# Values of the first attention issued for three key tiles at a time, with six tiles of probabilities held

## The chip, the cores and the metric

One Trainium2 chip, one of its cores. The metric is the device time of one execution in microseconds (us). It is told as the median of several runs, and one execution of its own is profiled.

## The reference

Four sequences x of 256 rows by 512 columns (float32), each with a context of 1601 rows by 512 columns, go through four residual steps:

```
x = x + latent_attention(layernorm(x), ctx)       # 16 heads of 32, low-rank: Wq_d, W_qk, Wkv_d, Wv_u
x = x + layernorm(x) @ dequantised_int4(W0).T + bias
x = x + grouped_attention(layernorm(x), ctx)      # 16 query heads of 96, 4 key/value heads
x = x + mixture(layernorm(x))                     # dense product plus a rank-32 path with expert weights
```

The change concerns the first step. There, for every head, scores = (C_q @ W_qk) @ C_kv^T / sqrt(32) over the 1601 context rows, attn = softmax(scores), and the result is attn @ C_kv @ Wv_u, with C_kv = ctx @ Wkv_d of 32 columns.

## The kernel before, in words

The program runs four blocks one after the other: products of the context, the latent attention with the quantised layer, the grouped attention, and the mixture. Only `latent_attention_and_ffn` (L663 to L1179) is touched.

It works in 16 stages, S = 4 sequences by 4 groups of 4 heads. A stage has 13 key tiles of 128 keys (the last has 65), and 1024 queries (4 heads by 256 rows) in two halves of 512 columns.

- TensorE, `scores(s, kt)` (L900): two matmuls with operands in fp32r (L909), one for each half, into one of three PSUM banks taken in turn (SB = 3). From the fourth half on it waits until the exponential of three halves earlier has read its bank (L908).
- ScalarE, `probs(s, kt)` (L1025): two exponentials (L1031), each from a bank into half of a tile of probabilities `pr`. There are NPR = 4 such tiles, and before tile n it waits for the values of tile n - NPR (L1028).
- TensorE, `values(s, kt)` (L914): two products with operands in float32 (L922), with 64 columns of `cv` as weights, one to partitions 0 to 63 and one to 64 to 127 of the same bank, summed over the stage. The trace shows each as two MATMUL records, so four for a tile.
- The rest of TensorE's work goes through a ring of four PSUM banks (`ring_item`, L956), whose banks are read by VectorE or ScalarE in the same order: 32 maxima of the next stages' scores a stage (L970 on TensorE in fp32r, L1132 on VectorE), the row of shifts (`row`, L974 and L93), and in some stages `raise` (L979), transposes (`xt`, `xat`, L952), `cq` (L989), `a` (L994), `ffn` (L1004), all these in float32, and `q` (L931, products in fp32r). An item is issued once the item four places earlier has been read.
- The order of all this on TensorE is written out by `course(s)` (L772): the scores of the first two units of key tiles, then by turns the values of a unit and the scores of the unit after the next. `some(share)` lays ring items in between, 2 shares after each tile's scores and 3 after a unit's values. `total` is the number of shares of a stage, so the items are spread evenly whatever the units are. ScalarE follows the same order (L1069), VectorE follows the ring items alone.

So TensorE runs a stage as: scores 0 to 3, values 0 and 1, scores 4 and 5, values 2 and 3, and so on, to scores 12, values 10 and 11, the row, values 12.

Of the kernel before, what the change touches and what calls it, by code (L numbers as in the profile page):

```python
# [97 lines left out]
def build(nc, A, out):  # L98
# [10 lines left out]
    with ExitStack() as ctx:  # L109
        def sb(name, shape, dt=F32):  # L110
            return ctx.enter_context(nc.sbuf_tensor(name, shape, dt))

        ident = sb("ident", [P, P])
        negid = sb("negid", [QT, QT])
        ps = ctx.enter_context(nc.psum_tensor("ps", [P, 8 * BANK], F32))
        ln = {n: sb(f"ln_{n}", s) for n, s in
              (("st", [P, TT, 6]), ("mv", [P, TT, 2]), ("v", [P, TT]), ("t", [P, TT]), ("u", [P, TT]), ("y", [P, TT]))}
        h8all = sb("h8all", [P, B, NE])
        dlall = sb("dlall", [P, B, NE])
        w1T = sb("w1T", [P, DC, D])  # L120
        with ExitStack() as early:
            def weight(name, cols, dt=F32R):
                return early.enter_context(nc.sbuf_tensor(name, [P, DC, cols], dt))

            wkvh, wkvl = weight("wkvh", WV + WK), weight("wkvl", WV + WK)
            wqh, wql = weight("wqh", H1 * HD1), weight("wql", H1 * HD1)
            w0T = weight("w0T", D, F32)
            small = {n: early.enter_context(nc.sbuf_tensor(n, shape, F32)) for n, shape in
                     (("bias0", [P, D]), ("wqd", [P, DC, LQ]), ("wqk", [LQ, H0, 3 * HD0]), ("wvu", [P, NG * 2, 2, HD0 + 1]),
                      ("xa", [P, TT, D]), ("cq", [LQ, T]))}  # L130
            context_products(nc, A, ident, negid, ps, ln, wkvh, wkvl, wqh, wql, w0T, w1T, *small.values(),
                             k_scr, v_scr, cst_scr, cv_scr, wo_scr)
            latent_attention_and_ffn(nc, A, ident, negid, ps, ln, wkvh, wkvl, wqh, wql, w0T, *small.values(),
                                     cst_scr, cv_scr, q_scr, k_scr, v_scr, x_scr)
        grouped_attention(nc, A, ident, negid, ps, ln, q_scr, k_scr, v_scr, x_scr, y_scr, z_scr, wo_scr, w1T,
                          h8all, dlall)
        mixture(nc, A, ident, ps, y_scr, z_scr, h8all, dlall, out)
# [525 lines left out]
def latent_attention_and_ffn(nc, A, ident, negid, ps, ln, wkvh, wkvl, wqh, wql, w0T, bias0, wqd, wqk, wvu, xa, cq,  # L663
# [10 lines left out]
    keys = [P] * (KT - 1) + [last_rows]  # L674
    cuts = widths(NC, 4)
    NI = QT * len(cuts)
    UNITS = [(0, 1), (2, 3), (4, 5), (6, 7), (8, 9), (10, 11), (12,)]
    NPR = 4
    LEAD = 6
    NQ, NKL = H1 * HD1 // T, -(-WK // T)  # L680
    NU = NQ + NKL + TT
# [3 lines left out]
    with ExitStack() as ctx:  # L685
        def sb(name, shape, dt=F32):
            return ctx.enter_context(nc.sbuf_tensor(name, shape, dt))
# [12 lines left out]
        ast = sb("ast", [HD1 + QT, H0 * T], F32R)  # L700
        pr = sb("pr", [P, NPR, GC])
        osb = sb("osb", [P, BANK])
# [20 lines left out]
        def bank(i, n=BANK):  # L723
            return ps[:, i * BANK:i * BANK + n]
# [47 lines left out]
        def course(s):  # L772
            main, row, tail = beside(s)
            taken, given = [0], []
            total = 2 * KT + 3 * (len(UNITS) - 2)

            def some(share):
                taken[0] += share
                out = main[len(given):len(main) * taken[0] // total]
                given.extend(out)  # L780
                return out

            for t in UNITS[0]:
                yield "scores", s, t
                yield from some(2)
            for j, unit in enumerate(UNITS):
                for t in UNITS[j + 1] if j + 1 < len(UNITS) else ():
                    yield "scores", s, t
                    yield from some(2)
                for t in unit:  # L790
                    yield "values", s, t
                if j < len(UNITS) - 2:
                    yield from some(3)
                if j == len(UNITS) - 2:
                    assert len(given) == len(main)
# [103 lines left out]
        def _(pe):  # L899
# [14 lines left out]
            def values(s, kt):  # L914
# [5 lines left out]
                for half in range(2):  # L920
                    pe.wait_ge(exp_done, 2 * n + half + 1)
                    mm = pe.matmul(bank(OB)[64 * half:64 * half + 64, :], cv[0:keys[kt], b % 2, kt, :],  # L922
                                   pr[0:keys[kt], n % NPR, half * BANK:(half + 1) * BANK],
                                   start=(kt == 0), stop=(kt == KT - 1))
# [99 lines left out]
        def _(act):  # L1024
            def probs(s, kt):  # L1025
                n = s * KT + kt
                if n >= NPR:
                    act.wait_ge(av_mm, n - NPR + 1)  # L1028
                for half in range(2):
                    act.wait_ge(s_mm, 2 * n + half + 1)  # L1030
                    act.activation(pr[0:keys[kt], n % NPR, half * BANK:(half + 1) * BANK],  # L1031
                                   bank((2 * n + half) % SB)[0:keys[kt], :], ACT.Exp, scale=S0).then_inc(exp_done, 1)
# [792 lines left out]
```

## Time and profile before

| what | us |
|---|---|
| median of 3 runs | 2090.02 (2086.51 to 2091.49) |
| the profiled execution's own time | 2088.55 |
| its span, first to last instruction | 2086.8 |
| latent attention, its 16 stages | about 346 to 952 of the span |
| TensorE busy, whole span | 1940.6 |
| ScalarE busy, whole span | 948.3 |
| VectorE busy, whole span | 1119.8 |

Busy times are of one engine each and overlap. Matmuls are pipelined, so their recorded lengths overlap too. In a timeline, therefore, the time that a group of matmuls takes is read from its start to the start of the next group.

### The profile page before, as it was taken

What the parts mean: (1) busy time and instruction counts of PE and PEld (TensorE: products, weight loads), DVE (VectorE), ACT (ScalarE), POOL (GpSimd) and SP (SyncE); (2) the same over time, 40 slices, a digit from 0 to 9 for tenths busy, and PEclk for the clock granted to TensorE, in tenths of its full rate; (3) what the DMA queues carried; (4) which work ended last, traced back from release to release, by engine and by line L of the source; (5) the groups of instructions that cost most, each with busy time, mean ns of one, the idle gap of its engine ahead of it and who ended that gap; (6) DMA issues with size and microseconds to landing.
All of it is one profiled execution on the core that took longest, in us unless ns stands there. A gap on an engine that the chain in (4) does not pass through costs nothing. (4 is left out here: it accounts for less than half of the span.)

```text
span 2086.8 us, 23683 instructions
## 1 busy us (share of the span) xinstructions
PE 1940.6 (93%) x8690; PEld 1363.5 (65%) x8690; DVE 1119.8 (54%) x2093; ACT 948.3 (45%) x1826; POOL 652.4 (31%) x504
## 2 busy tenths in 40 slices
PE   6999989999999999996799999999999999999986
PEld 5999975444655555554567777677776677766752
DVE  2443326767656656642374555666556466664423
ACT  2322312444443444341256666646666566655540
POOL 0000000000000000000156676656766567655650
PEclk9999986999999999998789999999999999999985
DMA  6556731000101100010721222213222332202112
GB/s 179 161 175 205 234 105 39 1 12 16 64 25 34 51 31 16 31 41 26 190 56 43 71 73 73 74 44 84 62 64 60 84 84 62 69 16 55 36 26 95
DMA packets 109697, 149.51 MB, mean 72 GB/s; under 512 B 28777, under 2 KB 87529, under 8 KB 106510
## 3 DMA queue, kind: packets, MB, share of 16 engines
q1 hardware_dynamic: 101630, 145.36, 24.3%
q10 hardware_dynamic: 7952, 2.64, 0.6%
q8 instruction: 69, 1.13, 0.2%
q14 instruction: 46, 0.38, 0.1%
HBM read 96.52 MB, written 51.39 MB: 71 GB/s over the span
## 5 line engine op out<-in xcount | busy, mean ns | idle before, releaser
L1365 POOL TENSOR_TENSOR pl<-pf,ph 128x512 fp32r<-128x512 f32 (+1 forms) x480 | 640.1, 1352 | 350.2 <-ACT pf L1532 348.5
L1528 ACT ACTIVATE ph<-ps 128x512 fp32r<-128x512 f32 (+1 forms) x480 | 287.3, 599 | 350.8 <-PE ps L1436 350.0
L1591 DVE TENSOR_REDUCE pm<-ps 128x1 f32<-128x464 f32 (+1 forms) x512 | 320.9, 637 | 157.0 <-PE ps L1382 148.6
L1132 DVE TENSOR_REDUCE pm<-ps 128x1 f32<-128x400 f32 (+1 forms) x512 | 264.3, 569 | 99.8 <-PE ps L970 96.9
L1031 ACT ACTIVATE pr<-ps 128x512 f32<-128x512 f32 (+1 forms) x416 | 219.4, 601 | 192.8 <-PE ps L909 191.6
L1532 ACT ACTIVATE pf<-ps 128x512 f32<-128x512 f32 (+1 forms) x480 | 287.2, 598 | 2.4 <-POOL pl L1365 2.2
L1382 PE MATMUL ps<-kh,qh 96*128 96x464 f32 (+1 forms) x512 | 203.5, 404 | 21.0 <-DMA ql<-q_scr 12.9
L1354 POOL MEMSET vf<- 128x96 f32 x1 | 0.2, 178 | 708.3 <-POOLq L685 708.3
L1454 PE MATMUL ps<-pl,vh 128*97 128x512 f32 (+1 forms) x480 | 194.7, 406 | 20.9 <-POOL pl L1365 19.7
L922 PE MATMUL ps<-pr,cv 128*64 128x512 f32 (+1 forms) x832 | 207.2, 614 | 0.0
L1451 PE MATMUL ps<-ph,vh 128*97 128x512 f32 (+1 forms) x480 | 195.7, 408 | 4.8 <-ACT ph L1528 4.8
L1434 PE MATMUL ps<-qh,kh 104*128 104x512 f32 (+1 forms) x480 | 193.8, 404 | 1.4 <-issue 1.4
L1435 PE MATMUL ps<-qh,kl 96*128 96x512 f32 (+1 forms) x480 | 191.5, 399 | 0.0
L970 PE MATMUL ps<-cst,ast 96*128 96x400 f32 (+1 forms) x512 | 175.8, 403 | 16.4 <-DVE pm L1132 12.2
L1436 PE MATMUL ps<-ql,kh 96*128 96x512 f32 (+1 forms) x480 | 190.3, 396 | 0.0
L1452 PE MATMUL ps<-ph,vl 128*97 128x512 f32 (+1 forms) x480 | 189.6, 395 | 0.0
L970 PEld LDWEIGHTS ps<-cst,ast 96*128 96x128 f32 x512 | 96.5, 201 | 109.5 <-DVE pm L1132 46.8
L909 PE MATMUL ps<-ast,cst 104*128 104x512 f32 (+1 forms) x416 | 153.1, 431 | 5.5 <-ACT pr L1031 2.0
L1382 PEld LDWEIGHTS ps<-kh,qh 96*128 96x128 f32 x512 | 100.3, 196 | 64.5 <-DVE pm L1591 25.9
L1596 DVE SCALAR_TENSOR_TENSOR x<-ps,rec,x 128x512 f32<-128x512 f32 x128 | 96.0, 750 | 80.6 <-PE ps L1395 80.4
L1454 PEld LDWEIGHTS ps<-pl,vh 128*97 128x97 f32 (+1 forms) x480 | 78.2, 163 | 76.8 <-POOL pl L1365 47.5
L922 PEld LDWEIGHTS ps<-pr,cv 128*64 128x64 f32 (+1 forms) x832 | 51.6, 138 | 85.5 <-issue 58.3
(222 smaller groups left out, 2655.4 us busy)
## 6 DMA issues: line engine op xcount, KB each, us to landing
woT<-wo_turned SPq DMA_DIRECT2D x16, 1536.0 KB, 8.8
cnat<-in_ctx_dram SPq DMA_DIRECT2D x16, 768.0 KB
q_scr<-qst SPq DMA_DIRECT2D x48, 256.0 KB, 2.5
kf<-k_scr SPq DMA_DIRECT2D x16, 696.4 KB, 4.8
vf<-v_scr SPq DMA_DIRECT2D x16, 672.0 KB
v_scr<-vst SPq DMA_DIRECT2D x64, 144.0 KB, 2.2
k_scr<-kst SPq DMA_DIRECT2D x36, 192.0 KB, 4.6
wo_turned<-wo_out SPq DMA_DIRECT2D x32, 192.0 KB, 2.8
```

The source lines that it names most:

```text
L922: mm = pe.matmul(bank(OB)[64 * half:64 * half + 64, :], cv[0:keys[kt], b % 2, kt, :], pr[0:keys[kt], n % NPR, half * BANK:(half + 1) * BAN ...
L970: mm = pe.matmul(out[:, 0:k], ast[0:HD1, grp * GC + j * P:grp * GC + (j + 1) * P], cst[0:HD1, b % 2, k0:k0 + k], start=True, stop=True)
L1031: act.activation(pr[0:keys[kt], n % NPR, half * BANK:(half + 1) * BANK], bank((2 * n + half) % SB)[0:keys[kt], :], ACT.Exp, scale=S0).then ...
L1132: dve.reduce_max(pm[:, j, ch:ch + 1], src[:, 0:cuts[ch][1]], AX).then_inc(done["dve"], 1)
L1365: pool.tensor_tensor(pl[0:m, n % 2, cols], pf[0:m, half, :], ph[0:m, n % 2, cols].bitcast(F32), ALU.subtract).then_inc(plo, 1)
L1382: mm = pe.matmul(at[:, 0:k], qh[0:HD1, a % 3, j * P:(j + 1) * P], kh[0:HD1, a % 3, k0:k0 + k], start=True, stop=True)
L1434: pe.matmul(out, kh[:, s % 3, k0:k0 + m], qh[:, s % 3, cols], start=True, stop=False)
L1451: pe.matmul(out, vh[0:m, s % 2, kt, :], ph[0:m, n % 2, cols], start=(kt == 0), stop=False)
L1454: mm = pe.matmul(out, vh[0:m, s % 2, kt, :], pl[0:m, n % 2, cols], start=False, stop=(kt == KT - 1))
L1528: act.activation(ph[0:keys[kt], n % 2, cols], src, ACT.Exp, scale=S1).then_inc(phi, 1)
L1532: act.activation(pf[0:keys[kt], half, :], src, ACT.Exp, scale=S1).then_inc(exp_done, 1)
L1591: ins = dve.reduce_max(pm[:, j, ch:ch + 1], at[:, 0:cuts[ch][1]], AX)
```

## The change

The key tiles are cut into units of three in place of two, and `pr` has six tiles in place of four. Nothing else is edited. `total` in `course` becomes 35 in place of 41, since it is worked out from the number of units.

```
-    UNITS = [(0, 1), (2, 3), (4, 5), (6, 7), (8, 9), (10, 11), (12,)]
-    NPR = 4
+    UNITS = [(0, 1, 2), (3, 4, 5), (6, 7, 8), (9, 10, 11), (12,)]
+    NPR = 6
```

TensorE's order in a stage is now: scores 0 to 5, values 0 to 2, scores 6 to 8, values 3 to 5, scores 9 to 11, values 6 to 8, scores 12, values 9 to 11, the row, values 12. As an example, the main part of stage 5 in both orders (S scores, V values, m a maximum):

```
before  S0 m S1 m raise S2 m S3 m m V0 V1 m m S4 m S5 m m V2 V3 m m S6 xt m S7 xt V4 V5 m m S8 m m S9 q V6 V7 m m m S10 m ...
after   S0 m S1 m raise S2 m m S3 m m S4 m S5 m m V0 V1 V2 m m m S6 xt m S7 xt S8 m m V3 V4 V5 m m q S9 m m S10 m ...
```

## Rows read from the trace of the kernel before

**Rows 1.** The page: busy time by engine, and granted clock in 40 slices.
```profile
PE 1940.6 (93%) x8690; PEld 1363.5 (65%) x8690; DVE 1119.8 (54%) x2093; ACT 948.3 (45%) x1826; POOL 652.4 (31%) x504
...
PEclk9999986999999999998789999999999999999985
```
**Rows 2.** Busy time of each engine in two stretches (us from the span's start).
```profile
345.00:952.00 607.00, 585.85 (x2684) 327.37 (x2686) 366.89 (x817) 262.72 (x501) 0.00 (x0) 0.98 0.09 28
...
927.00:930.50 3.50, 3.50 (x9) 0.89 (x6) 0.00 (x0) 0.78 (x2) 0.00 (x0) 0.52 0.01 4
```
**Rows 3.** Who waited for whom, 345 to 952: us in total, times, longest.
```profile
PEld ps L909 <- ACT pr L1031: 34.0, 79, 0.9
...
PEld ps L970 <- DVE qst L1175: 8.9, 11, 0.8
```
**Rows 4.** TensorE's timeline in a plain stage: start, length, instructions merged.
```profile
389.00 0.63 PE L970 MATMUL ps<-cst,ast 96*128 96x402 f32 x2
389.47 0.62 PE L909 MATMUL ps<-ast,cst 104*128 104x512 f32 x2
389.93 0.35 PE L970 MATMUL ps<-cst,ast 96*128 96x400 f32 x1
...
390.94 0.53 PE L970 MATMUL ps<-cst,ast 96*128 96x400 f32 x2
391.40 1.94 PE L922 MATMUL ps<-pr,cv 128*64 128x512 f32 x8
393.27 0.63 PE L970 MATMUL ps<-cst,ast 96*128 96x400 f32 x2
393.74 0.64 PE L909 MATMUL ps<-ast,cst 104*128 104x512 f32 x2
...
395.50 1.94 PE L922 MATMUL ps<-pr,cv 128*64 128x512 f32 x8
```
**Rows 5.** The same plain stage: timeline of TensorE's weight loads.
```profile
389.00 0.30 PEld L970 LDWEIGHTS ps<-cst,ast 96*128 96x128 f32 x2 [0.81 <-issue]
...
390.60 0.19 PEld L909 LDWEIGHTS ps<-ast,cst 104*128 104x128 f32 x1 [0.48 <-ACT pr L1031]
```
**Rows 6.** The same plain stage: timeline of ScalarE.
```profile
389.95 2.06 ACT L1031 ACTIVATE pr<-ps 128x512 f32<-128x512 f32 x4 [2.02 <-PE ps L909]
```
**Rows 7.** TensorE's timeline: values of the last tile alone, and what follows.
```profile
401.37 1.08 PE L922 MATMUL ps<-pr,cv 65*64 65x512 f32 x4
402.38 1.36 PE L970 MATMUL ps<-cst,ast 96*128 96x402 f32 x3
```
**Rows 8.** TensorE's timeline, stage 6: two maxima between scores.
```profile
576.39 0.53 PE L970 MATMUL ps<-cst,ast 96*128 96x400 f32 x2
576.75 0.39 PE L909 MATMUL ps<-ast,cst 104*128 104x512 f32 x1
```
**Rows 9.** TensorE's timeline, stage 7: a maximum ahead of a float32 item.
```profile
602.98 0.45 PE L970 MATMUL ps<-cst,ast 96*128 96x402 f32 x1
603.36 1.10 PE L994 MATMUL ps<-cq,wqk 64*96 64x256 f32 x4
```
**Rows 10.** TensorE's timeline, stage 6: a maximum ahead of an fp32r item.
```profile
567.78 0.45 PE L970 MATMUL ps<-cst,ast 96*128 96x400 f32 x1
568.07 0.67 PE L931 MATMUL ps<-xth,wqh 128*128 128x256 f32 x4
```
**Rows 11.** TensorE's timeline at the start of stage 1: first scores, first values.
```profile
374.65 0.62 PE L909 MATMUL ps<-ast,cst 104*128 104x512 f32 x2
...
378.92 1.94 PE L922 MATMUL ps<-pr,cv 128*64 128x512 f32 x8
```
**Rows 12.** TensorE's timeline at the start of stage 15, which has no maxima.
```profile
924.40 2.46 PE L909 MATMUL ps<-ast,cst 104*128 104x512 f32 x5 [0.47 <-ACT pr L1031]
926.79 3.38 PE L922 MATMUL ps<-pr,cv 128*64 128x512 f32 x8
930.10 1.16 PE L909 MATMUL ps<-ast,cst 104*128 104x512 f32 x3
```

## Prediction

> **What bounds the kernel now.** I read the page first [rows 1]. TensorE is busy for 93% of the span and ScalarE for 45%, and the granted clock is near full almost everywhere. The table by stretches then gives the part that the diff touches [rows 2]: in the 607 us from 345 to 952 TensorE has 585.85 us of recorded busy time, ScalarE 262.72, VectorE 366.89. So TensorE's own row of instructions sets the length of this part, and a change of order there is worth what it takes out of that row, less the waits that it puts in. Recorded lengths overlap and hide short waits (L922 x8 is recorded as 1.94 us but the next group starts 1.87 us later), so I price everything from start to start. The table of waits says whom TensorE waits for [rows 3]: 79 weight loads of scores waited for ScalarE's exponentials, and 11 loads of maxima for VectorE's part of a `q` item.
>
> **The change, part 1: fewer visits to the values.** A stage now goes to the values 5 times in place of 7, so 2 x 16 = 32 visits less over the 16 stages. The values themselves stay. A visit costs more than its products, in three places.
> - Inside: two tiles take 391.40 to 393.27 = 1.87 us [rows 4], one tile takes 401.37 to 402.38 = 1.01 us [rows 7]. A further tile therefore costs 0.86 us, and what is left, 1.01 - 0.86 = 0.15 us, is fixed.
> - Entry: two maxima ahead of values take 390.94 to 391.40 = 0.46 us [rows 4]. Ahead of scores they take 576.39 to 576.75 = 0.36 us [rows 8]. That is 0.10 us.
> - Exit: two maxima behind values take 393.27 to 393.74 = 0.47 us [rows 4], against the same 0.36: 0.11 us.
>
> Together 0.36 us for a visit, so 32 x 0.36 = 11.5 us less.
>
> The row of weight loads shows why the exit costs something [rows 5]: after the last values the load unit is idle for 0.81 us, and the next load starts only at 389.00, together with its matmul, and not under the values. The Trainium skill's page "TensorE: Matmul & The Clock Gate", section "Step-by-step: what each phase is for", says that TensorE pulls weight loads ahead of matmuls in flight, so the next weights load while the present ones are used. By that rule the exit would be free, and with it most of the gain would go. The trace does not agree at this place. The skill's page "TensorEngine Tiling (Array Packing)", section "Key Properties", says that changing the tiling mode drains the engine, which fits the idle 0.81 us but names no size.
>
> **Part 2: float32 items that lose their neighbour.** Written out, the order before goes from an fp32r product to float32 work 162 times over the part and its ends, 112 of them at values. The new one does so 143 times, 80 of them at values. So other float32 items enter on their own 63 times in place of 50: 13 more, since they now stand in the middle of scores rather than beside values. An entry costs 602.98 to 603.36 = 0.38 us for one maximum [rows 9] against 567.78 to 568.07 = 0.29 us ahead of an fp32r item [rows 10]: 0.09 us. 13 x 0.09 = 1.2 us more.
>
> **Part 3: scores wait for ScalarE.** Three banks hold the scores. The first exponential starts 389.95 - 389.47 = 0.48 us after the first scores [rows 4, 6], four take 2.06 us with their last recorded length of about 0.6, so one follows another in 0.48 us. The load of the fourth half could start only at 390.60 [rows 5], 1.13 us after the first scores. So half k (from 0) of a run of scores cannot start before 1.13 + 0.48 x (k - 3) us. From the fourth half to the values, with two maxima between, it is 391.40 - 390.60 = 0.80 us.
> - A unit in the middle. Before, 389.00 to 393.27 = 4.27 us with 5 maxima, 393.27 to the next values at 395.50 plus 1.87 = 4.10 us with 4 [rows 4]. At the average of 4.44 ring items (41 shares, 26 maxima) that is 4.17 us, for three tiles 6.26. After, three tiles have 6.7 items: two or three maxima behind the values (0.47 or 0.65 us), then the sixth half at 1.13 + 2 x 0.48 = 2.09 us, then 0.80 us, then 1.87 + 0.86 = 2.73 us of values. That is 6.09 with two and 6.27 with three, 6.13 at the mean number. A unit of three thus gains 0.13 us where visits alone would give half a visit, 0.18 us. The waits take 0.05 us, twice a stage: 0.1 us.
> - The start of a stage. Before, four tiles of scores stand there in one row; in stage 1 that is 374.65 to 378.92 = 4.27 us with `raise` in it [rows 11]. After, six stand there. The two tiles that join come at ScalarE's pace, 4 x 0.48 = 1.92 us, where their own products and three maxima would take 4 x 0.23 + 3 x 0.18 = 1.46 us (0.23 is half of 389.47 to 389.93 [rows 4], 0.18 half of the 0.36 above). The wait is up to 0.46 us, of which some 0.26 us was paid before as well, when scores 4 and 5 were a unit of their own and their fourth half started at 390.60 in place of 389.93 + 0.18 + 0.23 = 390.34.
>
> The start thus takes up to 0.20 us more. So waits add 0.1 to 0.3 us a stage, and where long items fill the row, nothing. I take 2 us for 16 stages (0.12 each), nearer to the low end since most stages have such items. Bounds: 0, if the items cover it; 16 x 0.6 = 10 us, if both the whole 0.46 us at the start and 0.07 us in each unit come on top.
>
> **Part 4: items of four banks.** VectorE reads a `q` item 0.59 + 0.69 us after its products, and values directly behind it covered that. In stages 5, 9 and 13 the first two `q` items are followed by values before, and by maxima or scores after: 6 items that lose this cover. A wait of this kind costs 0.8 us at most [rows 3]. Bounds 0 and 6 x 0.8 = 4.8 us; I take 1 us, since scores and waits for ScalarE stand between the item and the one four places later.
>
> **What is free.** Six tiles of probabilities cost no time; they keep ScalarE's wait at L1028 from binding, since tile n - 6 has been used before tile n is scored. `copy_o`, the row and the stores keep their places. VectorE has 366.89 us in 607 and four banks of slack; where it is late, behind the layernorms at the starts of stages 5, 9 and 13, TensorE waits in both orders. If that cover were gone, it would be in the bounds of part 3.
>
> **Sum.** -11.5 + 1.2 + 2 + 1 = -7.3 us. Against the profiled execution, whose time is 2088.55 us (span 2086.8), that is 2081.2. The median of the runs shown is 2090.02, 1.5 us above it, and against the median, to which the forecast is given, it is 2090.0 - 7.3 = 2082.7 us. A difference of less than 0.2% (4.2 us) can hardly be told from no change in this kernel.
>
> **Rivals.**
> 1. *The forecast*: visits saved, waits small. 2077 to 2085.8 us. Chance 0.53.
> 2. *Scores wait more.* Three banks and a longer run of scores: the gain goes back to ScalarE. With 0.5 us a stage in place of 0.12 the waits are 8 us and the sum is -11.5 + 1.2 + 8 + 1 = -1.3: 2088.7 us. For it: 79 waiting loads already [rows 3], 5 fp32r halves in a row started 0.49 us apart in stage 15 [rows 12]. Against: ScalarE has rested 2.02 us before the unit [rows 6], so it starts each one with all banks free. Chance 0.26.
> 3. *More is gained.* VectorE catches up during 2.73 us of values, and the waits of maxima shrink by 4 us with parts 3 and 4 at 0: -11.5 + 1.2 - 4 = -14.3, 2075.7 us. Chance 0.09.
> 4. *The clock falls in the run of six*, the case on the slower side. At the start of stage 15, where no maxima fill the scores, it stood at 0.52 in 927 to 930.5 [rows 2], the 1.2 GHz level, right after a run of scores at ScalarE's pace. The values took 926.79 to 930.10 = 3.31 us in place of 1.87 [rows 12]: 1.44 us. If it fell in every stage, that is 15 x 1.44 = 21.6 us and 2104.3. It decides from (7.3 + 4.2) / 1.44 = 8 stages on. Against it: the maxima keep TensorE fuller in all other stages, and the mean over the whole part is 0.98 [rows 2]. Chance 0.05 for slower. Stage 15 alone, up or down by 1 us, is in the range.
> 5. *Nothing is gained*, since the price of a visit is not fixed but lies under other waits: 2090 us, give or take 1.5. Against it: the 1.87 and 1.01 us. Chance 0.07.
>
> **How the numbers follow.** Faster by over 0.2%: rivals 1 and 3, 0.62. Within 0.2%: 2 and 5, 0.33. Slower: 0.05. The range leaves out half of rival 3, rival 4 and the upper edge of 5: 2076.5 to 2090.5 us. The likeliest case alone has 2077 to 2085.8.
>
> **What the profile after would show.** L922 in groups of twelve with 2.73 us to the next start; L970 behind values still 0.11 us longer; idle load unit of 0.81 us before 5 and no longer 7 loads a stage; the part from first to last exponential shorter by some 7 us, with the other parts as they were. The waits of L909 for L1031 should stay near 34 us. The prediction is wrong if these grow by over 5 us, if the fixed part of a visit grows with the number of its tiles, or if the clock falls at more stage starts than before.

## The result, and the profile after

The changed kernel takes 2105.8 us (median of 4 runs, 2103.4 to 2111.6) against 2089.97 for the kernel before. The ratio is 1.0082, with a 95% interval of 1.0056 to 1.0108. It is slower by about 16 us, where 2082.7 was forecast, with a range up to 2090.5. Its profiled execution took 2103.83 us, with a span of 2101.9.

The page of the changed kernel, where the lines of [rows 1] have become these, with the granted clock in 40 slices below:
```profile
PE 1945.8 (93%) x8690; PEld 1370.5 (65%) x8690; DVE 1117.3 (53%) x2093; ACT 944.8 (45%) x1826; POOL 651.3 (31%) x504
...
PEclk9999986999999999998779999999999999999985
```
The totals say nothing: the counts are the same and the shares differ by a point at most. The time went into the latent attention. I took the start of each stage's first exponential (L1031) from ScalarE's timeline. From the first of stage 0 to the last of stage 15 it is 603.3 us before and 617.2 after, 13.9 of the 15.1 us by which the spans differ. By stage, in us:

| stages | before | after | difference, sum |
|---|---|---|---|
| 0, 1, 3, 7, 11 (no layernorm) | 29.25, 28.93, 30.48, 39.43, 39.45 | 28.63, 28.49, 30.31, 38.83, 38.79 | -2.5 |
| 2, 4, 8, 12 (layernorm from `raise` at the start) | 35.32, 42.05, 42.11, 42.07 | 37.20, 45.21, 44.82, 45.13 | +10.8 |
| 5, 9, 13 (layernorm from `ffn` at the start) | 41.82, 42.83, 42.90 | 43.45, 43.47, 43.56 | +2.9 |
| 6, 10 (layernorm from `raise` at the start) | 42.96, 42.89 | 43.50, 43.40 | +1.1 |
| 14, 15 (no layernorm either) | 35.35, 25.47 | 35.75, 26.62 | +1.6 |

The five stages of the first row, which have no layernorm of VectorE beside them, got shorter. Stages 14 and 15 have none either and got longer: stage 14 by 0.40 us, stage 15 by 1.15. The loss, 14.8 us, is in the nine that have one, above all in 2, 4, 8 and 12.

Each time by stage is of one profiled execution. How far such times carry is shown by four more kernels that keep the order of before in the stages concerned (e1, e10, e11 and e12 below): their stages 2, 4, 6, 8, 10 and 14 agree with before within 0.1 us. Stages 0, 5, 9, 13 and 15, and once stage 12, differ by up to 1.7 us, with where the granted clock stood low. Stage 15 took 23.82 us in all four, without a fall of the clock, against 25.47 before; and with the units of the changed kernel it took 23.33 us in e9 and e13, without a fall, against 26.62. So what stage 15 lost in the table is a fall of the clock in that execution, and not its order.

How the loss arises can be seen at the start of stage 4. This is the timeline of the kernel before, TensorE and VectorE together (start, length, instructions merged, and in brackets the idle time before them):
```profile
471.85 0.71 PE L909 MATMUL ps<-ast,cst 104*128 104x512 f32 x2
...
473.38 0.69 DVE L67 BATCH_NORM_STATS2 ln_st<-x 128x6 f32<-128x512 f32 x1
473.70 0.52 PE L970 MATMUL ps<-cst,ast 96*128 96x400 f32 x2
...
474.15 1.94 PE L922 MATMUL ps<-pr,cv 128*64 128x512 f32 x8
...
475.79 1.06 DVE L1132 TENSOR_REDUCE pm<-ps 128x1 f32<-128x400 f32 x2
476.02 0.85 PE L970 MATMUL ps<-cst,ast 96*128 96x402 f32 x2
```
And the same place of the changed kernel:
```profile
474.33 0.71 PE L909 MATMUL ps<-ast,cst 104*128 104x512 f32 x2
...
475.85 0.70 DVE L67 BATCH_NORM_STATS2 ln_st<-x 128x6 f32<-128x512 f32 x1
...
476.26 0.77 PE L909 MATMUL ps<-ast,cst 104*128 104x512 f32 x2
...
478.26 1.05 DVE L1132 TENSOR_REDUCE pm<-ps 128x1 f32<-128x400 f32 x2
478.89 1.18 PE L970 MATMUL ps<-cst,ast 96*128 96x400 f32 x2 [1.86 <-DVE pm L1132]
...
481.55 4.62 PE L922 MATMUL ps<-pr,cv 128*64 128x512 f32 x12
...
486.10 0.81 PE L970 MATMUL ps<-cst,ast 96*128 96x400 f32 x3
```
VectorE begins its layernorm (L67) 1.5 us after the third tile's scores and reads no ring bank until 475.79 or 478.26, 2.4 us later. Before, TensorE has the values of tiles 0 and 1 in that time, which need nothing of VectorE, and comes back at 476.02 to free banks. After, two more tiles of scores and their maxima stand first. TensorE runs onto the full ring and is idle for 1.86 us. Then the values, at last issued, take 481.55 to 486.10 = 4.55 us instead of 2.73: the record of the granted clock has 0.5 from 478.4 to 485.3.

The table by stretches has the first 12 us of stages 2, 4 and 5 and then stages 0 to 14 as a whole. The columns are the stretch, its length, the busy time of TensorE, its weight loads, VectorE, ScalarE and GpSimd with their instructions, then granted clock, DMA share and GB/s. Before:
```profile
404.10:416.10 12.00, 10.74 (x47) 5.35 (x45) 11.19 (x36) 6.27 (x12) 0.00 (x0) 1.00 0.00 1
469.90:481.90 12.00, 10.62 (x47) 5.39 (x45) 11.18 (x36) 6.27 (x12) 0.00 (x0) 1.00 0.36 62
511.90:523.90 12.00, 9.28 (x35) 5.07 (x35) 11.31 (x35) 4.99 (x10) 0.00 (x0) 0.86 0.11 44
345.90:923.70 577.80, 558.25 (x2565) 313.82 (x2564) 364.10 (x809) 248.32 (x473) 0.00 (x0) 0.98 0.09 28
```
After:
```profile
404.80:416.80 12.00, 9.87 (x38) 5.20 (x38) 11.17 (x36) 6.20 (x12) 0.00 (x0) 0.87 0.01 1
472.30:484.30 12.00, 10.05 (x37) 5.78 (x37) 11.18 (x36) 6.20 (x12) 0.00 (x0) 0.76 0.33 61
517.60:529.60 12.00, 8.21 (x32) 5.61 (x32) 11.30 (x36) 6.32 (x12) 0.00 (x0) 0.86 0.11 44
347.70:938.30 590.60, 560.03 (x2565) 318.26 (x2564) 362.38 (x809) 246.04 (x474) 0.00 (x0) 0.97 0.09 27
```
In these 12 us VectorE is the busy engine (11.2 us), not TensorE, whatever the 607 us as a whole say. TensorE gets through 38 and 37 matmuls where it did 47. And in stages 2 and 4 the clock is no longer 1.00. In the record of the granted clock the part has 20.5 us at the lower level (1.2 GHz) before, in four stretches, and 37.5 us after, in eight. To these, in both, come the first 4.4 us of stage 0, where every run has 2.5 to 4.5 us at the lower level; here and below they are left out.

The table of waits of the changed kernel, 345 to 968, answers to [rows 3]:
```profile
PEld ps L909 <- ACT pr L1031: 38.7, 108, 0.9
...
PE ps L970 <- DVE pm L1132: 18.7, 10, 2.6
...
PE ps L931 <- DVE pm L1132: 4.0, 2, 2.0
```
The row of the kernel before, 345 to 952:
```profile
PE ps L970 <- DVE pm L1132: 12.2, 14, 2.6
```
So TensorE's own idle time before maxima was 12.2 us in 14 waits; now it is 18.7, and 4.0 before `q` items in stages 6 and 10.

What the change was to do, it did. TensorE's timeline in stage 6 of the changed kernel:
```profile
571.70 0.53 PE L970 MATMUL ps<-cst,ast 96*128 96x400 f32 x2
572.16 2.79 PE L922 MATMUL ps<-pr,cv 128*64 128x512 f32 x12
574.89 0.62 PE L970 MATMUL ps<-cst,ast 96*128 96x402 f32 x2
575.35 0.66 PE L931 MATMUL ps<-xth,wqh 128*128 128x256 f32 x4
```
Three tiles of values take 2.73 us, and the two maxima ahead of them and the two behind take 0.46 us each, where two within fp32r work take 0.36 [rows 8]. The fixed part of a visit is what it was and doesn't grow: 3 x 0.86 + 0.15 = 2.73 us.

### The profile page after: what moved, and what is told of

It reads as the page before. It is cut to its first block and busy times, and to the rows that moved or that the text cites. A ratio compares the mean times of both kernels' runs of the same rounds, so it can differ in the third digit from the quotient of the medians.

```text
span 2101.9 us, 23681 instructions
## 1 busy us (share of the span) xinstructions
PE 1945.8 (93%) x8690; PEld 1370.5 (65%) x8690; DVE 1117.3 (53%) x2093; ACT 944.8 (45%) x1826; POOL 651.3 (31%) x504
## 5 line engine op out<-in xcount | busy, mean ns | idle before, releaser
L1031 ACT ACTIVATE pr<-ps 128x512 f32<-128x512 f32 (+1 forms) x416 | 217.6, 611 | 163.4 <-PE ps L909 162.2
L970 PE MATMUL ps<-cst,ast 96*128 96x400 f32 (+1 forms) x512 | 171.1, 403 | 24.5 <-DVE pm L1132 18.7
L909 PE MATMUL ps<-ast,cst 104*128 104x512 f32 (+1 forms) x416 | 158.9, 442 | 5.4 <-ACT pr L1031 3.8
L1382 PEld LDWEIGHTS ps<-kh,qh 96*128 96x128 f32 x512 | 99.9, 195 | 63.7 <-DVE pm L1591 25.7
```

Of the source, the lines that this page charges most:

```text
L970: mm = pe.matmul(out[:, 0:k], ast[0:HD1, grp * GC + j * P:grp * GC + (j + 1) * P], cst[0:HD1, b % 2, k0:k0 + k], start=True, stop=True)
L1382: mm = pe.matmul(at[:, 0:k], qh[0:HD1, a % 3, j * P:(j + 1) * P], kh[0:HD1, a % 3, k0:k0 + k], start=True, stop=True)
```

## The experiments

Theory A was that the loss is at the starts of stages with a layernorm, by the run of six tiles of scores. Its rival B was that scores wait longer for ScalarE wherever units are of three, and C that the larger buffers cost time. "The part" is from the first to the last exponential of the 16 stages.

**Where in the stage.** Four sets of units, on the kernel before with NPR = 6:
```
e1_npr6        UNITS as before
e2_start6      [(0, 1, 2), (3, 4, 5), (6, 7), (8, 9), (10, 11), (12,)]
e3_late3       [(0, 1), (2, 3), (4, 5, 6), (7, 8, 9), (10, 11), (12,)]
e4_late3_five  [(0, 1), (2, 3), (4, 5, 6), (7, 8, 9), (10, 11, 12)]
```


> Six tiles of probabilities with the units of two as before. Theory A (the loss is at the starts of stages: with six tiles of scores in a row, TensorE runs onto a ring item while VectorE is in a layernorm, where the values of tiles 0 and 1 stood before, and the clock falls in that wait): same as before, 2090 within 4 us. Theory C (the larger buffer itself costs, by its place in memory or ScalarE's wait): 2100 to 2106 us.

Measured: 2087.97 us, ratio 0.9989 (0.9978 to 1.0), the part 603.3 us. The buffers cost nothing; C is out.

> The units of three only at the start of the stage (six tiles of scores in a row), pairs behind; six visits to the values. Theory A: the loss at the starts stays whole (some 25 us against the saved visits), 6 visits save 5.8 us, so 2103 to 2111 us. Theory B (the loss is spread over the units of three, as longer waits of scores for ScalarE's exponentials): about 2090 to 2095 us, since most units are pairs again.

Measured: 2110.41 us, ratio 1.0092 (1.0073 to 1.0112), within what A expects. The part is 624.7 us, 54.6 of them at the lower clock level.

> Start of the stage as before (four tiles of scores, then values 0 and 1), then two units of three, then (10, 11) and 12; six visits. Theory A: the loss is gone and one visit a stage is saved at 0.36 us: 2090 - 5.8 + 1 = 2085 us (2081 to 2088). Theory B: 2095 to 2101 us.

Measured: 2111.29 us, ratio 1.0090 (1.0066 to 1.0114). Theory A as stated falls: the start has its four tiles, and the kernel is as slow as e2. It is also 10 us above the upper end of what B expected.

> Start of the stage as before, then three units of three, the last of them tiles 10 to 12; five visits, as many as in the changed kernel. Theory A: 2090 - 11.5 + 2 = 2080.5 us (2076 to 2085), a saving of 0.36 us a visit. Theory B: 2098 to 2106 us. If the price of a visit is not real, 2090.

Measured: 2099.62 us, ratio 1.0038 (1.0019 to 1.0056). By the time A is wrong, and B has it in its range. The stages tell more. In e4, stages 0, 1, 3, 7 and 11 take 27.62, 27.91, 30.41, 38.08 and 38.17 us, 5.35 us less than before together (3.7 without stage 0, whose clock differs), so B, by which units of three lose wherever they stand, is wrong there. Stages 2, 4, 8 and 12 take 39.50, 45.75, 46.19 and 45.21, 15.1 us more, though they start with four tiles. TensorE's and VectorE's timeline in stage 2 of e4:
```profile
406.22 1.94 PE L922 MATMUL ps<-pr,cv 128*64 128x512 f32 x8
...
408.12 1.05 DVE L1132 TENSOR_REDUCE pm<-ps 128x1 f32<-128x400 f32 x2
408.75 0.93 PE L970 MATMUL ps<-cst,ast 96*128 96x400 f32 x2 [0.60 <-DVE pm L1132]
...
410.30 0.45 PE L970 MATMUL ps<-cst,ast 96*128 96x400 f32 x1 [0.62 <-DVE pm L1132]
...
415.55 3.68 PE L922 MATMUL ps<-pr,cv 128*64 128x512 f32 x8
```
From 408.12 on the layernorm goes on for another 6 us, with pauses in which VectorE reads two banks each. Through all of it TensorE gets two ring items in some 1.55 us (408.12 to 409.67 from pair to pair of maxima), unless values fill the time. In the kernel before a second pair of values stands in this stretch; here three tiles of scores and their maxima do, and the next values come at 415.55, at half clock. So it is not the run of six alone. Why e3, with six visits, is slower than e4 with five, was not looked into. Theory D: **under a layernorm of VectorE any order with more ring items between two visits to the values loses, by waits and then by the clock.** The next runs test it.

**The layernorms taken away.** In both kernels each `layernorm` inside `latent_attention_and_ffn` is left out and a copy of its input, scaled by 1.0, stands in its place; the three pauses stayed:
```
+def layernorm_left_out(...):
+    for _ in range(3):
+        pause()
+    ...
+        last = dve.tensor_scalar(out[:, i, :], x[:, i, :], 1.0, None, ALU.mult)
```


> The kernel before, but the layernorms inside the 16 stages are left out: each is one scaled copy of its input by 1.0, with the same three pauses at which VectorE reads ring items. It is the base for the next kernel. Theory D (the loss lies where VectorE is in a layernorm: TensorE then crawls at VectorE's pace unless values fill the time, and the granted clock falls): TensorE's waits of maxima shrink and the clock falls in the part go from 20 us at the lower level to under 10; some 12 to 20 us less than before, about 2072 to 2080 us.

Measured: 2053.69 us. The fall is larger than expected. Some of it lies outside the part, since the layernorms behind the last stage are left out too: what follows the last exponential takes 1126.7 us in place of 1137.5. The part takes 579.7 us, and behind the low start of stage 0 the clock doesn't fall in it.

> The changed kernel with the same layernorms left out in the same way. Theory D: no longer slower than its base; the saved visits show, 3 to 10 us less than the kernel before without layernorms. Theory B (longer waits for ScalarE in runs of three and six): 8 to 16 us more than that base, as in the full kernels.

Measured: 2055.12 us (2053.55 to 2058.21, against 2050.6 to 2055.78). The 16 us of difference have gone: the two can hardly be told apart. Inside the part, 576.8 against 579.7, the units of three are 2.9 us faster. That is what the saved visits are worth net by these two executions, and 1.0 us of it is in stage 0, where the clock stood low for 2.9 us in place of 4.5. The whole time doesn't show it, where 3 to 10 us less were expected. Waits for ScalarE may explain a share: 119 loads of scores waited for it, 84 without the change (345 to 925), and TensorE itself was idle before scores for 3.8 us in place of 2.0.

**Ring banks read sooner.** Two more pauses in each layernorm:
```
     chain.link(dve.bn_stats(st[:, 0, :], x[:, 0, :]))
+    early()
     chain.mark(dve.bn_stats(st[:, 1, :], x[:, 1, :]))
+    early()
```


> The kernel before, with two more pauses in each layernorm of the stages, one behind each of the two BATCH_NORM_STATS2, so VectorE reads four more ring items early in the layernorm. Theory D: ring banks come free earlier, TensorE waits less at the starts of stages 4, 5, 8, 9, 12 and 13, 2 to 8 us less: 2082 to 2088 us. Theory B: the same as before, 2090.

Measured: 2086.65 us, ratio 0.9987 (0.9964 to 1.0009): not told from no change. Stages 9 and 13 got 3.1 and 2.2 us shorter, stage 2 got 2.9 longer, with a fall of the clock, and stages 4, 8 and 12, which were to gain, got 0.6 to 0.9 longer.

> The changed kernel with the same two more pauses. Theory D: most of the loss goes, since TensorE no longer runs dry behind the full ring: 2080 to 2094 us, and less time at the lower clock level than the 37 us of the changed kernel. Theory B: 2100 to 2106 us.

Measured: 2098.57 us, ratio 1.0032 (1.0019 to 1.0046). By the medians it gets back 7 of the 16 us, less than expected, and the time at the lower level, which was to shrink, grew to 47.8 us of the part. So this expectation failed. Reading earlier also lengthens the layernorm: from its first instruction to its last it takes 10.1 us in stage 4, where it took 8.2. The time lies between what D and B expected, so these two runs decide nothing between them.

**The clock by itself.** Idle products keep TensorE busy in the waits. Each repeats the first half of the next tile's scores into the bank that it goes to anyway, and signals nobody:
```
+            def keep_busy(s, kt, times):
+                n, (b, g) = s * KT + kt, divmod(s, NG)
+                pe.wait_ge(exp_done, 2 * n - SB + 1)
+                for _ in range(times):
+                    pe.matmul(bank((2 * n) % SB)[0:keys[kt], :], ..., start=True, stop=True)
...
                     if w[0] == "scores":
                         scores(s, w[2])
+                        if s in (2, 4, 8, 12) and w[2] == 4:
+                            keep_busy(s, 5, 8)
```


> The changed kernel with eight idle products behind the scores of tile 4 in stages 2, 4, 8 and 12, just before TensorE waits for a ring bank: each repeats the first half of tile 5's scores into the bank that they go to anyway. They do nothing for the result and only keep TensorE busy in a wait of about 1.9 us. Theory D with the clock as the larger part of the loss: the clock no longer falls in these four stages, and they get shorter by 1.5 to 3 us each, so 2094 to 2100 us. If the clock is not the cause but only TensorE's wait for VectorE: no stage gets shorter, 2103 to 2109 us.

Measured: 2098.81 us, ratio 1.0052 (1.0034 to 1.0071). Stages 2, 4, 8 and 12 take 35.64, 43.28, 43.29 and 43.32 us, 6.8 less than in the changed kernel, with no fall in them. So the clock is a cause by itself, and more work made these stages shorter. The 7 us by which the whole time fell are a poorer measure: elsewhere the clock still fell, stages 5, 6 and 10 took 5.0 us more in this execution, and stage 15, which had no fall this time, 3.3 us less.

> The kernel before with ten idle products behind the scores of tile 1 in stages 5, 9 and 13, where TensorE waits 2.6 us for a ring bank and the clock falls in the kernel before too. Theory D with the clock as a cause by itself: no fall in these stages, each shorter by 1 to 2.5 us, 2083 to 2088 us. Otherwise 2089 to 2092 us.

Measured: 2086.62 us, ratio 0.9988 (0.9977 to 1.0), as expected, though the time alone can hardly be told from no change. The stages can: 5, 9 and 13 take 41.63, 41.56 and 41.61 us, where they take 41.82 to 43.45 in the kernel before, e1 and e10. Behind the low start of stage 0 the clock doesn't fall in the 598.3 us of the part.

> The changed kernel with idle products in all nine stages with a layernorm: eight behind the scores of tile 4 in stages 2, 4, 6, 8, 10 and 12, ten behind the scores of tile 1 in stages 5, 9 and 13. If the clock is most of the loss: it no longer falls inside the part, which gets to about 600 us from first to last exponential (617 in the changed kernel, 603 before, 598 in the kernel before with its three waits filled), and the time to 2084 to 2091 us. If the clock is less than half of the loss: 2095 us or more, though it doesn't fall. Either way its distance to the kernel before with filled waits is what the waits cost net of the saved visits.

Measured: 2099.16 us, ratio 1.0036 (1.0024 to 1.0049). So the clock is not most of the loss; the time is as expected if it is less than half. But the clock did fall: a second wait of 1.85 us in stages 5, 9 and 13 was left unfilled, with a fall behind each, so this run wasn't yet the case without falls.

> The changed kernel with idle products in all nine stages with a layernorm, and in stages 5, 9 and 13 also in the second wait, behind the scores of tile 4 (eight). The clock should not fall inside the part. Stages 5, 9 and 13 then lose what the half clock cost them, some 1.7 us each against 45.1: the part gets to about 607 us and the time to 2092 to 2097 us. What is then left above the kernel before with filled waits (598.3 us in the part), some 9 us, is TensorE's waiting for VectorE net of the saved visits. If the time is under 2090, the clock was most of the loss after all.

Measured: 2097.15 us, ratio 1.0031 (1.0015 to 1.0047), just above what was expected. The part takes 608.9 us. Behind that low start the clock doesn't fall in stages 0 to 14; it does in stage 15, which took 26.01 us. That is why stages 0 to 14 are compared from here on. TensorE's timeline at the start of stage 4 of this kernel, where L918 are the idle products:
```profile
474.33 2.12 PE L918 MATMUL ps<-ast,cst 104*128 104x512 f32 x8
476.29 0.85 PE L978 MATMUL ps<-cst,ast 96*128 96x400 f32 x2
...
477.75 0.93 PE L978 MATMUL ps<-cst,ast 96*128 96x400 f32 x2 [0.15 <-DVE pm L1144]
478.61 2.79 PE L930 MATMUL ps<-pr,cv 128*64 128x512 f32 x12
481.34 1.00 PE L978 MATMUL ps<-cst,ast 96*128 96x400 f32 x3
```
The values take 478.61 to 481.34 = 2.73 us again. And these are stages 0 to 14 of the two filled kernels, the one before (574.5 us) and the changed one (582.9 us), in the table by stretches (the 1.00 is rounded: it has the low 3.6 and 2.6 us at the start of stage 0 in it):
```profile
346.50:921.00 574.50, 560.29 (x2595) 314.31 (x2594) 363.29 (x809) 248.03 (x474) 0.00 (x0) 1.00 0.09 28
```
```profile
347.10:930.00 582.90, 574.21 (x2667) 327.72 (x2666) 361.94 (x809) 245.84 (x474) 0.00 (x0) 1.00 0.09 28
```

TensorE spends 25.7 us on its twelve groups of idle products in e14 and 7.7 us on its three in e11, and is still idle for 0.5 and 6.6 us before maxima. So 26 us went by in waits for VectorE, filled or not, against 14, some 12 more.

**A version that gains.** Units of three in five stages where no layernorm stands:
```
+    THREES = [(0, 1), (2, 3), (4, 5, 6), (7, 8, 9), (10, 11, 12)]
+    units_of = lambda s: THREES if s in (0, 1, 3, 7, 11) else PAIRS
```


> Units of three, (0,1) (2,3) (4,5,6) (7,8,9) (10,11,12), only in stages 0, 1, 3, 7 and 11, which have no layernorm of VectorE beside them; the units of two of before in all others. Theory D: the five stages gain what they gained in the kernel with five late units, 5.3 us together, and the others stay: 2082 to 2087 us. If units of three cost something everywhere: 2090 or more.

Measured: 2084.21 us, ratio 0.9978 (0.9968 to 0.9989), as expected. Stages 14 and 15 kept their pairs. Stage 14 has no layernorm and yet took 35.6 to 36.3 us in every kernel that has units of three in it, against 35.35 with pairs, so "no layernorm" is not the whole rule; what else stands against it there was not looked into.

> The mixed units of stages 0, 1, 3, 7 and 11 and the ten idle products of stages 5, 9 and 13 together. Theory D: the two gains add, 2078 to 2083 us, faster than either kernel of this case.

Measured: 2078.43 us (2077.13 to 2081.33), ratio 0.9956 (0.9942 to 0.9971), the fastest kernel here that leaves nothing out. The gains add, as expected. The part takes 594.0 us; stages 1, 7 and 11, take 27.92, 38.04 and 38.07 us against 28.88, 39.45 and 39.39 in the kernel before with filled waits: 0.96, 1.41 and 1.32 us for two saved visits, or 0.5 to 0.7 us a visit where 0.36 was the price read from the rows. Stage 3 took 30.40 us against 30.47: two visits less gained nothing there. What the difference between stages comes from was not tried.

## Why the prediction was wrong

**Part 1, the visit's price: right as read from the rows, but its effect differs from stage to stage.** 1.87 and 1.01 us became 2.73 us for three tiles, entry and exit stayed at 0.10 us each. In stages 1, 3, 7 and 11, which the clock leaves alone, 8 visits less gave 1.9 us after, where 2.9 were priced, and 3.7 us in e4.

**Part 2** was not tried by itself.

**Part 3, waits for ScalarE: small, as said.** The load of scores waited 108 times in place of 79, and 38.7 us in place of 34.0 in total, just under the 5 us that the prediction named as a sign of being wrong. TensorE itself was idle before scores for 3.8 us in place of 2.0.

**Part 4, `q` items: real, and near the size taken.** Without layernorms, stages 5, 9 and 13 are still 0.9 us longer each (39.06, 39.13, 39.05 against 38.19, 38.11, 38.18), 2.8 us together. The table of waits of these stages puts 0.4 us of each 0.9 down to a bank with a `q` item, 1.2 us in all, where 1 was taken and 4.8 allowed. The rest there is waits for maxima and for ScalarE.

Parts 1 to 4 together are worth -2.9 us in the part by e5 and e6, or -1.9 without stage 0, against the -7.3 of the sum. The sign was right and the size less than half. This alone would have left the kernel within 0.2% of before: the prediction's gain was too large even without the step that failed. Where the rest of it went is open; by stages, 6 and 10 gained 1.0 and 1.2 us without layernorms, and 4, 8 and 12 gained 0.2 at most.

**"What is free": here it failed.** The step was that VectorE "has 366.89 us in 607 and four banks of slack", that behind layernorms "TensorE waits in both orders", and that a loss of this cover would be "in the bounds of part 3". It was not; the bounds of part 3 spoke of ScalarE. VectorE has slack over 607 us but next to none for 8 to 10 us in each of nine stages; the table by stretches has it busy for 11.2 to 11.3 of 12 us in stages 2, 4 and 5. Nor was it stages 5, 9 and 13 alone. In the kernels as they are, stages 2, 4, 8 and 12 cost most (10.8 us against 2.9); with the waits filled they cost 4.1 us and stages 5, 9 and 13 cost 5.6, since there the clock falls in the kernel before as well. Under the layernorms the values of tiles 0 to 3 were long work, 1.87 us a pair, that needs neither VectorE nor a free bank, and the change put more ring items ahead of them. The missing term, by differences of the part from first to last exponential:

| | before | after | after less before |
|---|---|---|---|
| as it is | 603.3 | 617.2 | +13.9 |
| waits filled, clock kept up, stages 0 to 14 (e11, e14) | 574.5 | 582.9 | +8.4 |
| as it is, stages 0 to 14 | 577.8 | 590.6 | +12.8 |
| layernorms left out (e5, e6) | 579.7 | 576.8 | -2.9 |
| layernorms left out, stages 0 to 14 | 555.8 | 553.3 | -2.5 |

So of +12.8 us in stages 0 to 14, the clock is 12.8 - 8.4 = 4.4. TensorE's waits under the layernorms are the rest and have also eaten the saved visits: 8.4 + 2.5 = 10.9 us, if the visits are worth the same with and without layernorms. The time in idle products and in waits left over, some 12 us more in e14 than in e11, was counted in another way and agrees with it to about a microsecond. The rows are of one execution each, in which stage 0 alone differs by up to a microsecond, and filler work may itself move a wait by some tenths, so this split is good to a microsecond or two. One thing was not separated: with fewer units `total` falls from 41 to 35 shares, so the ring items also stand closer together among the scores.

**The rivals.** The fourth, on the slower side, had the effect right and the place wrong. The clock did fall in more stages, but behind TensorE's waits for VectorE, not because scores at ScalarE's pace are too thin: stages 0, 1 and 3, which have the same run of six, show no fall beyond the low start of stage 0. Its reckoning also took the falls as the whole price, and they are a third. The one place it was drawn from, the start of stage 15, does not bear it out: the fall stood there in the kernel before and not in e1, e10, e11 and e12, with the same order of pairs, and in the changed kernel and e14 (6.8 us each) and not in e9 and e13, with the same order of threes. The second rival put the loss in waits for ScalarE, and e6 speaks against it.

## What to carry to other kernels

Independent work that looks like mere order may be the cover of another engine's long stretch. Before moving it, look at each engine's busy share in windows as short as the stretch, not over the whole part; an engine at 60% can be the bound for 10 us. Where an order is written by a rule for all stages, let the stages differ: units of three in five stages without a layernorm and pairs in the others gave 0.22%, and with idle work in three waits 0.44%. And before a time by stage is read off one execution, look at what the same stage takes in other kernels that leave it alone: here a fall of the clock that came and went moved stage 15 of the changed order by 3.3 us, as much as some of the differences that one wants to explain.

## What the runs showed of the hardware

- Ten idle products in a wait of 2.6 us made stages 5, 9 and 13 of the kernel before shorter: 41.6 us against 41.8 to 42.9, and the clock stayed at 1.00 (e11). Eight in a wait of 1.9 us took four stages of the changed kernel from 37.2, 45.2, 44.8 and 45.1 to 35.6, 43.3, 43.3 and 43.3 us (e9). A wait costs its length and then what the clock takes from the work behind it: 1.82 us on one group of twelve matmuls.
- At the lower level (1.2 GHz) the same group of values takes 4.55 us in place of 2.73. That is less than double: the clock is back at 1.00 at 485.3, and the group ends at 486.10.
- The clock fell in an idle stretch of TensorE of 1.86 us (changed kernel, 477.0 to 478.9; the lower level stands from 478.4), and after two waits of 0.60 and 0.62 us among short groups of matmuls (e4, stage 2; from 410.8).
